# Operands of a one-column threshold and of one normalisation moved from SBUF to PSUM on VectorE

## The chip, the cores and the metric

The kernel runs on one core of a Trainium2 chip. The metric is the device time of one execution in microseconds (us), lower is better.

## What is computed

The reference is one block of a transformer with modulation, on x of 8 x 1024 x 512 in fp32. Cut to what matters here:

```
mod = silu(c) @ wmod                       # six rows of 512 for each batch: sa, ca, ga, sb, cb, gb
h = layernorm(x) * (1 + ca) + sa
x = x + ga * attention(h)                  # 3 iterations, output only nonzero in a few rows (below)
h = layernorm(x) * (1 + cb) + sb
x = x + gb * (quantise(h) @ quantise(w).T + bias)

# attention, after each iteration it
diff = mean(abs(iter_out - prev))
attn_out = where(done, attn_out, iter_out)
done = done | (diff < thr + fac * diff) & (it > 0)
```

The reference slices the first 16 positions of each batch before it iterates, so attention works on 8 x 16 = 128 rows. All other rows get only a constant row from it.

## The kernel before

The work is in two strands that share the engines.

**The main strand.** The 8192 rows are cut into 64 tiles of 128 rows, in 16 groups of four (`TILES = 4`). ScalarE normalises (`normalise`, line 474) and sums; GpSimd multiplies and adds the modulation in half groups of 128 x 1024 (`times_c`, line 379; `plus_sb`, line 390) and takes the quantised values back from the grid (`from_grid`, line 366); VectorE finds the block maxima (1215) and puts values on the grid (1234). For each tile TensorE turns the values (`transposes`, line 724), ScalarE takes the high part of them (`high_part`, line 454), VectorE the low part (`low_part`, line 1196), and TensorE multiplies in 12 matmuls (`product`, line 746). VectorE multiplies the result by the gate (`times_gate`, line 1255) and adds it to x (`add_tile`, line 1261), and ScalarE then presets the freed PSUM bank with the bias (`preset`, line 463).

**The head.** The 128 attention rows are worked on in small steps between the tiles. Each engine has one loop, `for q in range(LAST)`, with q from 0 to 63, and calls `head_work(q)` in it. The passes of the attention are `attend(i, o)`: pass i (0 to 2), step o, with q = 9 + 15 i + o. After them comes the head's own second half, at q = `AFTER` + n with `AFTER` = 51.

**Order.** Every engine's order is written out by hand and engines wait for each other by semaphores. VectorE carries out its instructions in order: in each q it does `times_gate(q - 1)`, `low_part(q + 1)`, `add_tile(q - 1)`, the group's grid work, and last `head_work(q)`. So what `head_work(q)` takes delays the three tile steps of q + 1. TensorE's `transposes(n)` waits for `low_part(n - 2)`, in the loop of q = n - 2. `link` marks an instruction whose end VectorE waits for before the next.

**The places that the change touches.**

- *The threshold*, step o = 14 of pass 1, q = 38, lines 1129 to 1137. TensorE has summed the differences into column 0 of `bb` (PSUM bank 7). Four instructions on one column make `dn[:, 2]` (the mean difference), `dn[:, 3]` (the bound), `dn[:, 6]` (1 if the difference is under the bound) and `dn[:, 7]` (one less that). `dn` is in SBUF. The two flags are read in pass 2, o = 12 (lines 1121 and 1123). TensorE waits for `dn_step` in pass 2, o = 0, before it overwrites `bb`.
- *The head's second normalisation*, q = 55 and 56, lines 1173 to 1180. `xs` (SBUF, 128 x 512) holds the head's x, `bb` the projected attention, `msp` (SBUF) the modulation rows, `mv` mean and variance, `hs` (SBUF) the result, which `quantise` takes at q = 57. `xs` is read again by GpSimd at the end (line 431).
- `own` is PSUM bank 5, which holds VectorE's small scratch values.

Of the kernel before, what the change touches and what calls it, by code (L numbers as in the profile page):

```python
# [9 lines left out]
ALU = mybir.AluOpType  # L10
# [3 lines left out]
B, T, D = 8, 1024, 512  # L14
HEADS, HD, E, ITERS = 16, 32, 16, 3
# [22 lines left out]
def build(nc, x, xh, WqT, WkT, WvT, WoT, bo, lna, BDs, rows, columns, masks, w, bias, cT, wmod, ident, out):  # L38
# [4 lines left out]
    with ExitStack() as ctx:  # L43
# [94 lines left out]
        s64 = own[:, 0:64].rearrange("p (h n) -> p h n", h=2)  # L138
        inv = own[:, 64:128].rearrange("p (h n) -> p h n", h=2)
        rsp, lmax, ksum, qrs = own[:, 128:128 + TILES], own[:, 144:160], own[:, 160:176], own[:, 176:192]  # L140

        def by_column(a):
            return a.rearrange("p (n b) -> p n b", b=B)
# [493 lines left out]
        def _(pe):  # L637
# [147 lines left out]
            def attend(i, o):  # L785
                if o == 0:
                    pe.wait_ge(q_ready, i + 1)
                    pe.wait_ge(kT_ready, i + 1)
                    M(ba, BD[:, 0, :], qT, start=True, stop=True).then_inc(qc_mm, 1)
                    if i == 0:  # L790
                        pe.wait_ge(cleared, 4)
                        pe.wait_ge(bd_done, 8)
                        pe.wait_ge(lrow_done, 5)
                    if i == 2:
                        pe.wait_ge(dn_step, 1)
                    project(bb, kT, 2, 1, kc_mm)
                elif o == 1:
                    pe.wait_ge(qc_cp, 2 * i + 2)
                    for c in range(NC):
                        m = M(ba[:, 4 * c:4 * c + 4], sq[:, 0, c * P:(c + 1) * P], col[:, GM:GM + 4],  # L800
                              start=True, stop=True)
                    m.then_inc(vq_mm, 1)
                elif o == 4:
                    pe.wait_ge(kn_done, i + 1)
                    turn(bb, kn, knT_mm)
                    pe.wait_ge(vT_ready, i + 1)
                    project(ba, vT, 3, 2, vn_mm)
                elif o == 6:
                    pe.wait_ge(knT_cp, i + 1)
                    pe.wait_ge(vn_cp, i + 1)  # L810
                    M(ba, mkr[:, 0:P], mkr[:, P:P + D], start=True, stop=False, skip_group_check=True)
                    logits(i, 0)
                    if i < ITERS - 1:
                        M(bb, BD[:, 1, :], kT, start=True, stop=True).then_inc(kv_mm, 1)
                    logits(i, 1)
                elif o == 7:
                    logits(i, 3)
                elif o == 8 and i < ITERS - 1:
                    pe.wait_ge(kT_ready, i + 2)
                    M(bb, BD[:, 3, :], vT, start=True, stop=True).then_inc(kv_mm, 1)  # L820
                elif o == 11:
                    pe.wait_ge(eT_done, i + 1)
                    if i < ITERS - 1:
                        pe.wait_ge(vT_ready, i + 2)
                    for h in range(HEADS):
                        for j in range(4):
                            r = slice(32 * j, 32 * j + 32)
                            m = M(bb[r, 32 * h:32 * h + 32], eT[r, h % 4, h // 4, :], vn[r, 32 * h:32 * h + 32],  # L828
                                  start=True, stop=True)
                    m.then_inc(pv_mm, 1)  # L830
                elif o == 13 and i < ITERS - 1:
                    pe.wait_ge(ai_done, i + 1)
                    turn(ba, cur[i], aiT_mm)
                    if i == 1:
                        pe.wait_ge(dsum_done, 1)
                        M(bb[:, 0:1], ones[:], dn[:, 0:1], start=True, stop=True).then_inc(dsum_mm, 1)
# [81 lines left out]
        def _(dve):  # L918
# [5 lines left out]
            def link(ins):  # L924
                ins.then_inc(dve_step, 1)
                chain[0] += 1
                dve.wait_ge(dve_step, chain[0])
# [134 lines left out]
            def moments(src, n):  # L1062
                link(W_.bn_stats(bn[:], src))
                link(W_.bn_aggr(mv[:], bn[:]))
                TS(st[:, 0, n:n + 1], mv[:, 1:2], EPS, None, ALU.add).then_inc(var_done, 1)
# [6 lines left out]
            def attend(i, o):  # L1072
# [14 lines left out]
                elif o == 8:  # L1087
                    dve.wait_ge(lg_mm, 4 * i + 4)
                    TT(lg, ba.rearrange("p (q c t) -> p q c t", q=4, c=NC),
                       st[:, 4, 0:16].rearrange("p (c q) -> p q c", q=4).unsqueeze(3).to_broadcast([P, 4, NC, 32]),  # L1090
                       ALU.mult).then_inc(lg_step, 1)
                    flat = lg.rearrange("p q c t -> p (q c) t")
                    dve.wait_ge(lg_step, 2 * i + 1)
                    RED(lmax, flat, AX, ALU.max).then_inc(lg_step, 1)
                    dve.wait_ge(lg_step, 2 * i + 2)
                    TT(flat, flat, wide16(lmax), ALU.subtract).then_inc(sub_done, 1)
                elif o == 10:
                    dve.wait_ge(ex_done, i + 1)
                    W_.transpose(eT.rearrange("p q c t -> p (q c t)"),
                                 ex.rearrange("p q c t -> p (q c t)")).then_inc(eT_done, 1)  # L1100
                    RED(st[:, 6, 0:16], ex.rearrange("p q c t -> p (q c) t"), AX, ALU.add).then_inc(e_step, 1)
                    dve.wait_ge(e_step, 2 * i + 1)
                    REC(st[:, 7, 0:16], st[:, 6, 0:16]).then_inc(e_step, 1)
                elif o == 12:
                    dve.wait_ge(e_step, 2 * i + 2)
                    dve.wait_ge(pv_mm, i + 1)
                    held = bb.rearrange("p (c q d) -> p c q d", c=NC, q=4)
                    scale = st[:, 7, 0:16].rearrange("p (q c) -> p c q", q=4).unsqueeze(3).to_broadcast([P, NC, 4, HD])
                    if i == 1:

                        TT(held, held, scale, ALU.mult).then_inc(diff_done, 1)
                        dve.wait_ge(diff_done, 1)
                        W_.tensor_copy(cur[1], bb).then_inc(ai_done, 1)
                        TT(diff, bb, cur[0], ALU.subtract).then_inc(diff_done, 1)
                        dve.wait_ge(diff_done, 2)
                        RED(dn[:, 0:1], diff, AX, ALU.add, apply_absolute_value=True).then_inc(dsum_done, 1)
                    else:
                        TT(cur[i].rearrange("p (c q d) -> p c q d", c=NC, q=4), held, scale, ALU.mult).then_inc(ai_done, 1)
                        dve.wait_ge(ai_done, i + 1)
                    if i == 2:  # L1120
                        TS(bb, cur[1], dn[:, 6:7], None, ALU.mult).then_inc(keep_done, 1)
                        dve.wait_ge(keep_done, 1)
                        STT(att[:], cur[2], dn[:, 7:8], bb, ALU.mult, ALU.add).then_inc(att_done, 1)
                elif o == 14 and i < ITERS - 1:
                    dve.wait_ge(aiT_mm, i + 1)
                    TT(qT, chunked(ba), qT, ALU.add).then_inc(q_ready, 1)
                    if i == 1:
                        dve.wait_ge(dsum_mm, 1)
                        TS(dn[:, 2:3], bb[:, 0:1], 1.0 / (B * HEADS * T * HD), None, ALU.mult).then_inc(dn_step, 1)
                        dve.wait_ge(dn_step, 1)  # L1130
                        TS(dn[:, 3:4], dn[:, 2:3], col[:, FAC:FAC + 1], col[:, THR:THR + 1],
                           ALU.mult, ALU.add).then_inc(dn_step, 1)
                        dve.wait_ge(dn_step, 2)
                        TT(dn[:, 6:7], dn[:, 2:3], dn[:, 3:4], ALU.is_lt).then_inc(dn_step, 1)  # L1134
                        dve.wait_ge(dn_step, 3)
                        TS(dn[:, 7:8], dn[:, 6:7], -1.0, 1.0, ALU.mult, ALU.add).then_inc(dn_step, 1)
                        dve.wait_ge(dn_step, 4)

            def head_work(q):
                i, o = pass_of(q)  # L1140
# [29 lines left out]
                elif q == AFTER + 4:  # L1170
                    dve.wait_ge(head_mm, PROJECTED)
                    dve.wait_ge(msp2_in, 16 * B)
                    link(TT(bb, bb, msp[:, GA - 1, :], ALU.mult))
                    link(TT(xs[:], xs[:], bb, ALU.add))
                    moments(xs[:], 2)
                elif q == AFTER + 5:
                    dve.wait_ge(std_done, 3)
                    link(REC(st[:, 3, 2:3], st[:, 1, 2:3]))
                    link(STT(bb, xs[:], mv[:, 0:1], msp[:, C - 1, :], ALU.subtract, ALU.mult))  # L1179
                    link(STT(hs[:], bb, st[:, 3, 2:3], msp[:, SB - 1, :], ALU.mult, ALU.add))  # L1180
                elif q == AFTER + 6:
                    quantise(hs[:].unsqueeze(1), Qh[:].unsqueeze(1), NB).then_inc(sxd_done, 1)
# [200 lines left out]
```

## Time and profile before

| | us |
|---|---|
| median of 3 runs | 339.31 |
| lowest and highest | 336.63 and 339.8 |
| the profiled execution | 338.35 |
| its span, first to last instruction | 336.3 |
| busy in it: TensorE (matmul) | 304.5 (91%) |
| VectorE | 290.4 (86%) |
| ScalarE | 239.9 (71%) |
| GpSimd | 227.5 (68%) |
| mean granted TensorE clock | 0.974 of full |

The engines are named PE (TensorE, with PEld for its weight loads), DVE (VectorE), ACT (ScalarE), POOL (GpSimd). A timeline row gives start, duration, engine, line of the kernel, operation and operands as output<-inputs, and in brackets how long the engine had been idle before and what ended that. Times are us from the start of the span. Tile names are the program's: all PSUM banks are `ps`, and `early` holds qT.

### The profile page before, as it was taken

What the parts mean: (1) busy time and instruction counts of PE and PEld (TensorE: products, weight loads), DVE (VectorE), ACT (ScalarE), POOL (GpSimd) and SP (SyncE); (2) the same over time, 40 slices, a digit from 0 to 9 for tenths busy, and PEclk for the clock granted to TensorE, in tenths of its full rate; (3) what the DMA queues carried; (4) which work ended last, traced back from release to release, by engine and by line L of the source; (5) the groups of instructions that cost most, each with busy time, mean ns of one, the idle gap of its engine ahead of it and who ended that gap; (6) DMA issues with size and microseconds to landing.
All of it is one profiled execution on the core that took longest, in us unless ns stands there. A gap on an engine that the chain in (4) does not pass through costs nothing. (4 is left out here: it accounts for less than half of the span.)

```text
span 336.3 us, 6060 instructions
## 1 busy us (share of the span) xinstructions
PE 304.5 (91%) x2159; PEld 227.8 (68%) x2159; DVE 290.4 (86%) x512; ACT 239.9 (71%) x536; POOL 227.5 (68%) x122
## 2 busy tenths in 40 slices
PE   7879999785899989998999999996999998998993
PEld 5213547565798777786888678874787785776782
DVE  4678759979999799799989979999798899989753
ACT  3278845698679979799998989976799875322410
POOL 1449393599748886969999996977878967722100
PEclk9999998979699999999999999999799999999999
DMA  6999699999979839996899699964773693303133
GB/s 185 394 406 399 231 150 239 355 307 346 225 174 241 154 134 225 276 212 232 136 236 271 221 229 247 248 175 79 228 117 127 185 146 142 127 0 125 49 140 94
DMA packets 23971, 69.00 MB, mean 205 GB/s; under 512 B 2387, under 2 KB 2516, under 8 KB 19974
## 3 DMA queue, kind: packets, MB, share of 16 engines
q1 hardware_dynamic: 16304, 53.83, 48.0%
q0 software_dynamic: 7392, 14.68, 26.0%
q8 instruction: 17, 0.28, 0.3%
q10 hardware_dynamic: 246, 0.12, 0.2%
q14 instruction: 12, 0.10, 0.1%
HBM read 51.48 MB, written 17.14 MB: 204 GB/s over the span
## 5 line engine op out<-in xcount | busy, mean ns | idle before, releaser
L746 PE MATMUL ps<-WH,XH 128*128 128x512 f32 x256 | 108.8, 427 | 1.1 <-issue 0.9
L746 PE MATMUL ps<-WL,XH 128*128 128x512 f32 x256 | 103.3, 405 | 0.0
L379 POOL TENSOR_TENSOR U<-U,c_bc 128x1024 f32<-128x1024 f32 x31 | 74.6, 2408 | 39.0 <-ACT U L474 38.4
L390 POOL TENSOR_TENSOR U<-U,sb_bc 128x1024 f32<-128x1024 f32 x31 | 74.4, 2399 | 2.5
L746 PE MATMUL ps<-WH,XL 128*128 128x512 f32 x256 | 69.7, 394 | 0.2 <-DVE XL L1196 0.2
L463 ACT COPY ps<-bias_bc 128x512 f32<-128x512 f32 x61 | 36.0, 590 | 38.9 <-DVE X L1261 38.9
L1255 DVE TENSOR_TENSOR ps<-ps,gb_bc 128x512 f32<-128x512 f32 x64 | 44.3, 692 | 15.7 <-PE ps L746 15.6
L746 PEld LDWEIGHTS ps<-WH,XH 128*128 128x128 f32 x256 | 50.0, 195 | 11.0 <-ACT XH L454 2.0
L746 PEld LDWEIGHTS ps<-WL,XH 128*128 128x128 f32 x256 | 50.2, 196 | 10.2 <-issue 1.1
L746 PEld LDWEIGHTS ps<-WH,XL 128*128 128x128 f32 x256 | 48.9, 191 | 11.8 <-DVE XL L1196 0.7
L454 ACT ACTIVATE XH<-ps 128x512 fp32r<-128x512 f32 x64 | 37.5, 587 | 22.8 <-PE ps L724 22.7
L724 PE MATMUL ps<-idf,DD 128*128 128x128 f32 x256 | 40.1, 281 | 13.5 <-DVE DD L1243 6.9
L366 POOL TENSOR_TENSOR DD<-Q,s 128x1024 f32<-128x1024 fp8e4 x24 | 46.1, 1919 | 9.1 <-DVE Q L1234 9.1
L1196 DVE TENSOR_TENSOR XL<-ps,XH 128x512 fp32r<-128x512 f32 x64 | 43.6, 682 | 8.5 <-ACT XH L454 8.4
L474 ACT ACTIVATE U<-X,nmr,rstd 128x512 f32<-128x512 f32 x64 | 48.3, 808 | 3.0 <-DVE nmr L1208 2.6
L724 PEld LDWEIGHTS ps<-idf,DD 128*128 128x128 f32 x256 | 30.7, 144 | 22.9 <-issue 9.6
L498 ACT ACTIVATE unused<-X,negm 128x512 bf16<-128x512 f32 x64 | 45.6, 714 | 0.5
L1261 DVE TENSOR_TENSOR X<-ps,X 128x512 f32<-128x512 f32 x64 | 43.6, 681 | 0.1
L1234 DVE TENSOR_TENSOR Q<-U,ps 128x1024 fp8e4<-128x1024 f32 x32 | 38.9, 1216 | 1.7 <-issue 0.4
L487 ACT ACTIVATE unused<-X 128x512 bf16<-128x512 f32 x64 | 39.5, 621 | 0.9 <-POOL X L343 0.9
L1215 DVE TENSOR_REDUCE amax<-U 128x32 f32<-128x1024 f32 x32 | 38.8, 1211 | 0.0
L356 POOL DMA_DIRECT2D X<-mod_scratch x14 | 18.1, 1293 | 11.5 <-DMA X<-in_x 6.5
(212 smaller groups left out, 351.1 us busy)
## 6 DMA issues: line engine op xcount, KB each, us to landing
X<-in_x SPq DMA_DIRECT2D x16, 1024.0 KB, 8.6
out<-X SPq DMA_DIRECT2D x15, 1024.0 KB, 4.7
X<-mod_scratch POOLq DMA_DIRECT2D x14, 1024.0 KB, 10.9
X<-in_wmod SPq DMA_DIRECT2D x2, 1024.0 KB, 12.3
sb_bc<-mod_scratch SPq DMA_DIRECT2D x7, 256.0 KB, 8.0
c_bc<-mod_scratch SPq DMA_DIRECT2D x7, 256.0 KB, 6.6
gb_bc<-mod_scratch SPq DMA_DIRECT2D x7, 256.0 KB, 8.2
msp<-mod_scratch SPq DMA_DIRECT2D x8, 160.0 KB, 9.8
```

Source lines behind the costliest of these rows:

```text
L366: nc.gpsimd.tensor_tensor(blocks(DD[:, g % 2, HALF * h:HALF * (h + 1), :]), blocks(Q8[:, h]), s32[:, g % 2, h, :].unsqueeze(2).to_broadcas ...
L379: nc.gpsimd.tensor_tensor(a, a, spread(c_bc[:, b % 2, :]), ALU.mult).then_inc(u_done, 2 if g == 0 else 1)
L390: nc.gpsimd.tensor_tensor(a, a, spread(sb_bc[:, b % 2, :]), ALU.add).then_inc(h_done, 2 if g == 0 else 1)
L474: A.activation(U[:, g % 2, j, :], X1[:, g % XSLOTS, j, :], ACT.Identity, bias=nmr[:, g % 2, j:j + 1], scale=rstd[:, g % 2, j:j + 1]).then_ ...
L487: A.activation(unused[:, j % 2, :], X1[:, g % XSLOTS, j, :], ACT.Identity, accum_out=total[:, j:j + 1]).then_inc(sum_done, 1)
L498: A.activation(unused[:, j % 2, :], X1[:, g % XSLOTS, j, :], ACT.Square, bias=negm[:, g % 2, j:j + 1], accum_out=ss[:, j:j + 1]).then_inc( ...
L724: m = TR(ps[:, XT_BANK + n % 2, c * P:(c + 1) * P], DD[:, g % 2, j, c * P:(c + 1) * P], idf[:])
L746: return M(bank, a[:, k * P:(k + 1) * P], w[:, k, :], start=False, stop=last, skip_group_check=n >= 3)
L1196: TT(XL[:, n % 2, :], ps[:, XT_BANK + n % 2, :], XH[:, n % 3, :].bitcast(F32), ALU.subtract).then_inc(xl_done, 1)
L1234: TT(blocks(Q8[:, h]), blocks(U[:, g % 2, HALF * h:HALF * (h + 1), :]), wide(inv[:, h, :]), ALU.mult, saturate=False).then_inc(q_done, 1)
L1255: TT(bank, bank, gb_bc[:, b % 2, :], ALU.mult).then_inc(scaled, 1)
L1261: TT(a, ps[:, Y_BANKS[n % 3], :], a, ALU.add).then_inc(o_done, 1)
```

## The change

Three columns of `own` get the names `change`, `bound` and `closer`. The threshold's difference is written twice, to `dn[:, 2]` and to `change`; the bound is computed from `change` into PSUM; the comparison has the bound as its tensor and `dn[:, 2]` as a per-partition scalar; its result goes to PSUM and a copy of it to `dn[:, 6]`. `dn_step` counts two more, and TensorE waits for 2 in place of 1. In the second normalisation the sum x + attention is written to `bb` in place of `xs`, its moments are taken from `bb`, a copy brings it to `xs`, and the first scalar_tensor_tensor reads `bb` in place of `xs`.

```diff
+        change, bound, closer = own[:, 400:401], own[:, 401:402], own[:, 402:403]
...
                     if i == 2:
-                        pe.wait_ge(dn_step, 1)
+                        pe.wait_ge(dn_step, 2)
                     project(bb, kT, 2, 1, kc_mm)
...
                         TS(dn[:, 2:3], bb[:, 0:1], 1.0 / (B * HEADS * T * HD), None, ALU.mult).then_inc(dn_step, 1)
-                        dve.wait_ge(dn_step, 1)
-                        TS(dn[:, 3:4], dn[:, 2:3], col[:, FAC:FAC + 1], col[:, THR:THR + 1],
-                           ALU.mult, ALU.add).then_inc(dn_step, 1)
+                        TS(change, bb[:, 0:1], 1.0 / (B * HEADS * T * HD), None, ALU.mult).then_inc(dn_step, 1)
                         dve.wait_ge(dn_step, 2)
-                        TT(dn[:, 6:7], dn[:, 2:3], dn[:, 3:4], ALU.is_lt).then_inc(dn_step, 1)
+                        TS(bound, change, col[:, FAC:FAC + 1], col[:, THR:THR + 1], ALU.mult, ALU.add).then_inc(dn_step, 1)
                         dve.wait_ge(dn_step, 3)
-                        TS(dn[:, 7:8], dn[:, 6:7], -1.0, 1.0, ALU.mult, ALU.add).then_inc(dn_step, 1)
+                        TS(closer, bound, dn[:, 2:3], None, ALU.is_gt).then_inc(dn_step, 1)
                         dve.wait_ge(dn_step, 4)
+                        W_.tensor_copy(dn[:, 6:7], closer).then_inc(dn_step, 1)
+                        TS(dn[:, 7:8], closer, -1.0, 1.0, ALU.mult, ALU.add).then_inc(dn_step, 1)
+                        dve.wait_ge(dn_step, 6)
...
                     link(TT(bb, bb, msp[:, GA - 1, :], ALU.mult))
-                    link(TT(xs[:], xs[:], bb, ALU.add))
-                    moments(xs[:], 2)
+
+                    link(TT(bb, bb, xs[:], ALU.add))
+                    moments(bb, 2)
                 elif q == AFTER + 5:
                     dve.wait_ge(std_done, 3)
                     link(REC(st[:, 3, 2:3], st[:, 1, 2:3]))
-                    link(STT(bb, xs[:], mv[:, 0:1], msp[:, C - 1, :], ALU.subtract, ALU.mult))
+                    link(W_.tensor_copy(xs[:], bb))
+                    link(STT(bb, bb, mv[:, 0:1], msp[:, C - 1, :], ALU.subtract, ALU.mult))
```

## Rows read from the trace of the kernel before

**Rows 1.** The page: granted clock in 40 slices, and the chain's shares by engine.

```profile
PEclk9999998979699999999999999999799999999999
PE 22%; DVE 9%; issue 3%; ACT 2%; DVEq 0%
```

**Rows 2.** The timeline around the threshold, 225 to 242 us.

```profile
225.82 0.15 DVE L1129 TENSOR_SCALAR dn<-ps 128x1 f32<-128x1 f32 x1
...
226.00 0.28 DVE L1131 TENSOR_SCALAR dn<-dn,col 128x1 f32<-128x1 f32 x1
226.06 2.37 POOL L379 TENSOR_TENSOR U<-U,c_bc 128x1024 f32<-128x1024 f32 x1 [2.15 <-ACT U L474]
226.31 2.13 DVE L1134 TENSOR_TENSOR dn<-dn 128x1 f32<-128x1 f32 x1
...
228.57 2.36 POOL L390 TENSOR_TENSOR U<-U,sb_bc 128x1024 f32<-128x1024 f32 x1
228.67 0.70 DVE L1255 TENSOR_TENSOR ps<-ps,gb_bc 128x512 f32<-128x512 f32 x1
...
230.01 0.66 PE L724 MATMUL ps<-idf,DD 128*128 128x128 f32 x4 [1.03 <-DVE XL L1196]
...
230.59 0.59 ACT L463 COPY ps<-bias_bc 128x512 f32<-128x512 f32 x1 [2.98 <-DVE X L1261]
...
235.97 1.18 PE L800 MATMUL ps<-col,sq 128*128 128x4 f32 x8 [2.56 <-ACT sq L508]
...
241.93 0.70 DVE L1255 TENSOR_TENSOR ps<-ps,gb_bc 128x512 f32<-128x512 f32 x1 [2.40 <-PE ps L746]
```

**Rows 3.** Stretches: length, then busy us (instructions) of PE, PEld, DVE, ACT, POOL, then granted clock, DMA share and GB/s.

```profile
118.00:122.00 4.00, 3.15 (x16) 2.69 (x17) 3.86 (x8) 3.14 (x9) 4.00 (x2) 1.00 0.48 190
...
237.00:240.00 3.00, 3.00 (x10) 2.55 (x11) 2.49 (x5) 2.97 (x8) 3.00 (x2) 0.50 0.85 236
```

**Rows 4.** The chain that ended last in order of time, 237 to 245 us.

```profile
237.15 0.95 PE ps L724 x4
238.10 3.79 PE ps L746 x12
241.89 0.44 PE ps L724 x4
242.33 2.77 PE ps L746 x12
```

**Rows 5.** The timeline around the second normalisation, 303 to 309 us.

```profile
303.47 2.50 DVE L1179 SCALAR_TENSOR_TENSOR ps<-xs,mv,msp 128x512 f32<-128x512 f32 x1
303.50 1.91 POOL L366 TENSOR_TENSOR DD<-Q,s 128x1024 f32<-128x1024 fp8e4 x1 [4.09 <-DVE Q L1234]
...
306.01 0.75 DVE L1180 SCALAR_TENSOR_TENSOR hs<-ps,st,msp 128x512 f32<-128x512 f32 x1
306.79 0.70 DVE L1255 TENSOR_TENSOR ps<-ps,gb_bc 128x512 f32<-128x512 f32 x1
...
308.14 0.66 PE L724 MATMUL ps<-idf,DD 128*128 128x128 f32 x4 [1.43 <-DVE XL L1196]
```

**Rows 6.** The timeline: VectorE instructions with a PSUM operand while GpSimd works.

```profile
119.76 2.42 POOL L390 TENSOR_TENSOR U<-U,sb_bc 128x1024 f32<-128x1024 f32 x1
...
120.84 0.23 DVE L1085 TENSOR_SCALAR st<-ps,tsc 128x16 f32<-128x16 f32 x1
...
216.59 1.91 POOL L366 TENSOR_TENSOR DD<-Q,s 128x1024 f32<-128x1024 fp8e4 x1
...
217.10 0.69 DVE L1113 COPY odd<-ps 128x512 f32<-128x512 f32 x1
```

**Rows 7.** TensorE's timeline: an earlier idle time of the engine.

```profile
118.85 0.66 PE L724 MATMUL ps<-idf,DD 128*128 128x128 f32 x4 [1.70 <-DVE XL L1196]
```

**Rows 8.** VectorE's groups by shape: busy us and mean ns after the bar.

```profile
L1063 DVE BATCH_NORM_STATS2 bn<-xs 128x6 f32<-128x512 f32 x2 | 1.4, 691 | 0.0
L1063 DVE BATCH_NORM_STATS2 bn<-ps 128x6 f32<-128x512 f32 x1 | 0.7, 699 | 0.0
```

## The prediction, made before the changed kernel ran

> **What bounds the kernel now.** I read the page first, then the chain of waits in order of time, then the timeline around the two places that the diff touches. TensorE is the engine that the kernel waits for: it has the largest share of the chain that ended last [rows 1], and where it stands still the time is lost for good, because one product follows the other up to the end of the span. So for each edit the question is whether TensorE stands still because of it. It does at both places.
>
> At the threshold a comparison of a single column takes 2.13 us, from 226.31 to 228.44. GpSimd's instruction began at 226.06 and took 2.37, so it ended at 228.43 [rows 2]. One column is no work (its neighbours take 0.15 and 0.28), so the comparison waited for GpSimd to finish. It is the only one of the four that reads two tensors from SBUF. Behind it on VectorE stand the gate product, the low part and the add of the next tile. TensorE stands still for 1.03 us until that low part is there, ScalarE for 2.98 until the add is, and as ScalarE is then late with the square that pass 2 needs, TensorE stands still again, for 2.56 until 235.97 [rows 2]. Then TensorE's clock falls to its lower level (0.50 granted, 1.2 GHz) between 237 and 240 [rows 3], and four transposes take 0.95 and a product's 12 matmuls 3.79 us, where those that follow take 0.44 and 2.77 [rows 4].
>
> At the second normalisation the scalar_tensor_tensor of two SBUF tensors takes 2.50 us; its twin with one PSUM tensor takes 0.75. GpSimd worked from 303.50 to 305.41. The low part behind it is late, and TensorE stands still for 1.43 [rows 5].
>
> **The change part by part: the threshold.** From the start of the first instruction to that of the next gate product it took 228.67 - 225.82 = 2.85 us [rows 2]. Afterwards there are six instructions.
> - The two that write the difference (`dn[:, 2]` and `change`) have no wait between them: 0.09 for the first and 0.18 for the second. The 0.18 is the distance from the first to the second start now, 226.00 - 225.82; the 0.09 is my estimate for one that is not waited for, half of that (bounds 0 and 0.18).
> - `bound`, with two per-partition scalars from SBUF, 0.31, the distance 226.31 - 226.00 [rows 2].
> - `closer`, with one per-partition scalar from SBUF and its tensor in PSUM: 0.23 plus 0.04 until the next start = 0.27. The nearest row is such an instruction on 16 columns, which took 0.23 while GpSimd was in the middle of an instruction (119.76 to 122.18) [rows 6]. So this form did not wait.
> - The copy to `dn[:, 6]`, 0.09, and the last, 0.19 (228.67 less the end of the comparison, 228.44, less 0.04 for the start).
>
> The sum is 0.09 + 0.18 + 0.31 + 0.27 + 0.09 + 0.19 = 1.13, so VectorE is free 2.85 - 1.13 = 1.72 earlier. Bounds: with each unwaited one at 0.18 it is 1.54; with them at nothing, 1.90.
>
> What does that give TensorE? The first idle time of 1.03 goes, as 1.72 is more. The other arrives through ScalarE: it waited 2.98 for the add and had nothing else to do, then worked without a break until the square, so all of this comes 1.72 earlier, and the matmuls at 235.97 start at 234.25. TensorE, which had won 1.03 before, now waits 2.56 - (1.72 - 1.03) = 1.87. The win at this point is 1.72. VectorE is no bound afterwards: at 241.93 it waits 2.40 for TensorE [rows 2].
>
> TensorE's wait for `dn_step` 2 in place of 1 costs nothing: TensorE has the rest of a product and the query projection ahead of this wait. If that cover were gone it would cost the 0.09 to 0.18 of the second write.
>
> **The clock.** It fell after an idle time of 2.56 and eight matmuls of 4 columns. With 1.87 in its place the nearest row is the idle time of 1.70 before 118.85 [rows 7], in a stretch whose clock stayed at 1.00 [rows 3], and there is the 1.43 before 308.14, where the page's slices show no fall either [rows 1, 5]. 1.87 is much nearer to 1.70 than to 2.56, so I take it that the clock stays up. What comes back is (0.95 - 0.44) + (3.79 - 2.77) = 1.53 us [rows 4]; bounds 0 (it falls all the same) and 1.53. It reaches the end, since the chain in these rows is TensorE's alone.
>
> **The second normalisation.** From 303.47 to the next gate product at 306.79 it took 3.32 [rows 5]. Afterwards: the copy of 128 x 512 from PSUM, 0.69 by its like, which did not wait though GpSimd was working from 216.59 to 218.50 [rows 6], plus 0.04 = 0.73; the first scalar_tensor_tensor, now with one SBUF tensor, 0.78 as its twin (306.79 - 306.01); and the twin itself, 0.78. The sum is 2.29 and the win 1.03. TensorE's idle time of 1.43 shrinks to 0.40, so all 1.03 arrives. Writing the sum to `bb` in place of `xs` at q = 55 costs nothing: it is one instruction with one PSUM and one SBUF tensor as before, and the moments cost 699 in place of 691 ns [rows 8]. The added copy is the price here; without it the win would be 1.76, of which TensorE could take 1.43.
>
> A rule of the Trainium skill speaks against the change: the page "VectorE: DVE Perf Modes", section "The TRN2 errata — SBUF-src ops pay a fixed extra latency per instruction", has 120 cycles fixed for a VectorE instruction from PSUM and 58 from SBUF, at 0.96 GHz. By it, as an estimate, the five instructions that change their source would each cost 0.065 us more, 0.32 in all. The rows show 8 ns for the moments from the one and the other [rows 8], so here the measurement decides.
>
> **The sum.** 1.72 + 1.53 + 1.03 = 4.28 us off the profiled execution's 338.35 (span 336.3 and 2.05 around it) gives 334.1. The median of the runs shown is 339.31, that is 0.96 above the profiled one, and with that the forecast is 335.0.
>
> **The rivals.**
> - *The clock falls all the same.* Both stalls go, but after the idle time of 1.87 and the eight matmuls the clock falls as it does now, or the runs' median did not have the loss to begin with (they differ by 3.2 us, and the fall may be part of that). For it: the idle time shrinks but does not go. Against it: 1.70 left the clock up [rows 3, 7]. The win is 2.75: 336.6.
> - *The win at the threshold doesn't arrive.* Something else is ready only later: GpSimd's next multiply waits for ScalarE and would come 1.72 earlier as well, but GpSimd's instruction before it lasts until 230.93 [rows 2]; a group's work that began late there would make the tiles of a later group late. Against it: TensorE and not GpSimd ended the waits between 237 and 245 [rows 4]. Then only 1.03 is left: 338.3.
> - *The other side: instructions with one tensor in SBUF wait as well.* Then at the threshold one of the small ones waits until 228.43 as now, and the next waits through GpSimd's following instruction, 228.57 to 230.93 [rows 2]: the gate product starts at about 231.1, 2.4 later. At the normalisation the copy takes the 2.50 and both others follow at 0.78 each, so 0.8 later than now. Together 3.2 slower: 342.5. It decides from the first instruction that waits; with no second wait it would be about even. Against it are both pairs of [rows 6]. The change then would not do what its wording says.
>
> **How the numbers follow.** Forecast 0.50, the clock falls all the same 0.33, the threshold's win doesn't arrive 0.13, the waits stay 0.04. The predicted time is the first case's, 335.0. By itself it spans 333.0 to 336.2: the unwaited instructions give 0.2 either way, and the median of a few runs whose times lie 3.2 apart moves by more than a microsecond. The range that leaves out no more than 2 in 10 reaches over the second and third case, 333.0 to 338.4. A change of 1% (3.4 us) is about what a measurement of this kernel can tell from none. Faster by over 1% is under 335.9: most of the first case (0.40) and a part of the second (0.09), 0.49. Slower by over 1% is the last case, 0.04. Within 1% is what remains, 0.47.
>
> **What the changed profile would show.** The comparison (`ps<-ps,dn`) at about 0.2 us with GpSimd in the middle of its multiply; no idle time of TensorE before the transposes that stood at 230.01; an idle time near 1.9 before the matmuls of line 800 in pass 2, and a granted clock of 1.00 behind it; products of 2.8 us there. Further on a copy of 0.69, two scalar_tensor_tensors of 0.75, and TensorE's idle time at 0.4 in place of 1.43. I would be wrong if one of the new instructions took 2 us, if TensorE's idle time moved to another place between 240 and 300, or if the granted clock still fell after pass 2 began.

## The result, and the profile after

| | before | changed |
|---|---|---|
| median, 20 executions each | 338.79 | 335.43 |
| lowest and highest | 336.63 and 339.83 | 332.6 and 339.02 |
| the profiled execution, its span | 338.35, 336.3 | 333.93, 331.9 |

The ratio of changed to before is 0.9896 (95% interval 0.9872 to 0.9921): 1% faster, 3.4 us between the medians. The ratio leaves out the changed kernel's three slowest executions (338.49 to 339.02) as slow ones; with them the means of the twenty are 338.5 and 335.6, 2.9 us apart. The profiled executions lie 4.4 us apart, and the changed kernel's times spread over 6.4 us where those of before spread over 3.2. TensorE's clock has a part in both facts, and the experiments below are mostly about it.

The timeline of the changed kernel at the threshold answers to [rows 2]:

```profile
225.77 0.15 DVE L1130 TENSOR_SCALAR dn<-ps 128x1 f32<-128x1 f32 x1
225.84 0.16 DVE L1131 TENSOR_SCALAR ps<-ps 128x1 f32<-128x1 f32 x1
...
226.02 2.38 POOL L380 TENSOR_TENSOR U<-U,c_bc 128x1024 f32<-128x1024 f32 x1 [2.18 <-ACT U L475]
226.03 0.28 DVE L1133 TENSOR_SCALAR ps<-ps,col 128x1 f32<-128x1 f32 x1
...
226.35 0.23 DVE L1135 TENSOR_SCALAR ps<-ps,dn 128x1 f32<-128x1 f32 x1
226.61 0.16 DVE L1137 COPY dn<-ps 128x1 f32<-128x1 f32 x1
226.69 0.15 DVE L1138 TENSOR_SCALAR dn<-ps 128x1 f32<-128x1 f32 x1
...
226.87 0.70 DVE L1259 TENSOR_TENSOR ps<-ps,gb_bc 128x512 f32<-128x512 f32 x1
...
227.87 1.05 PE L772 MATMUL ps<-BD,early 128*128 128x128 f32 x8
...
228.76 0.60 PE L725 MATMUL ps<-idf,DD 128*128 128x128 f32 x4
228.79 0.59 ACT L464 COPY ps<-bias_bc 128x512 f32<-128x512 f32 x1 [1.22 <-DVE X L1265]
...
234.17 1.05 PE L801 MATMUL ps<-col,sq 128*128 128x4 f32 x8 [2.06 <-ACT sq L509]
...
238.50 0.70 DVE L1259 TENSOR_TENSOR ps<-ps,gb_bc 128x512 f32<-128x512 f32 x1 [0.78 <-PE ps L747]
```

GpSimd works from 226.02 to 228.40, and all of the threshold's instructions but the first two start within that. The comparison (L1135) takes 0.23 us where it took 2.13. The way to the next gate product is 226.87 - 225.77 = 1.10 us where it was 2.85. TensorE has no idle time before the transposes at 228.76. Before line 801 it still stands idle, for 2.06 us.

The timeline at the second normalisation answers to [rows 5]:

```profile
300.01 0.69 DVE L1182 COPY xs<-ps 128x512 f32<-128x512 f32 x1
300.04 1.91 POOL L367 TENSOR_TENSOR DD<-Q,s 128x1024 f32<-128x1024 fp8e4 x1 [4.11 <-DVE Q L1238]
...
300.73 0.76 DVE L1183 SCALAR_TENSOR_TENSOR ps<-ps,mv,msp 128x512 f32<-128x512 f32 x1
...
301.53 0.75 DVE L1184 SCALAR_TENSOR_TENSOR hs<-ps,st,msp 128x512 f32<-128x512 f32 x1
...
302.31 0.70 DVE L1259 TENSOR_TENSOR ps<-ps,gb_bc 128x512 f32<-128x512 f32 x1
...
303.66 0.66 PE L725 MATMUL ps<-idf,DD 128*128 128x128 f32 x4 [0.41 <-DVE XL L1200]
```

The copy and the first scalar_tensor_tensor run in 0.69 and 0.76 us under GpSimd's instruction. It takes 2.30 from the copy to the next gate product where it took 3.32, and TensorE's idle time is 0.41 where it was 1.43.

### The profile page after: what moved, and what is told of

The parts are those of the page before. It is cut to its first block and busy times, and to the rows that moved or that the text cites. A ratio compares the mean times of both kernels' runs of the same rounds, so it can differ in the third digit from the quotient of the medians.

```text
span 331.9 us, 6063 instructions
## 1 busy us (share of the span) xinstructions
PE 302.6 (91%) x2159; PEld 226.5 (68%) x2159; DVE 287.5 (87%) x515; ACT 239.7 (72%) x536; POOL 227.4 (69%) x122
```

## The clock after pass 2 begins

The stretch from 230 to 246 us in this execution (columns as in [rows 3]) has no fall of TensorE's granted clock:

```profile
230.00:246.00 16.00, 13.94 (x77) 11.54 (x76) 14.93 (x30) 14.56 (x35) 13.85 (x8) 1.00 0.76 174
```

Three more executions of the changed kernel and one of before were profiled:

> The changed kernel itself, one look. In the profile shown, at 333.9, the granted clock stayed at 1.00 around 237 us. My theory (the same idle time of about 2 us is followed by a fall in some executions): an execution of 333 to 334 shows no fall there, one of 336 or more shows the clock at 0.50 for 3.4 or 6.9 us near 234 to 242. Rival (the slower executions differ elsewhere): an execution of 336 or more without a fall there.

> As the look before it, another execution: no fall and 333 to 334, or a fall near 234 to 242 us and 336 or more. The instructions of VectorE at the threshold and the normalisation take the same in both.

> As the two looks before it, a third execution: no fall and 333 to 334, or a fall near 234 to 242 us and 336 or more.

> The kernel before, one more look. My theory (after the longer idle time of 2.56 us the clock falls in nearly every execution, so that its times spread little): a fall to 0.50 near 237 us for 3.4 us or longer, at 337.5 to 340. Rival: no fall, and a time of 337 or less.

The changed kernel's three have two fences each here: from the timeline, TensorE's matmuls of line 801, and the stretch from 230 to 246 us. First execution:

```profile
236.36 1.05 PE L801 MATMUL ps<-col,sq 128*128 128x4 f32 x8 [2.05 <-ACT sq L509]
```

```profile
230.00:246.00 16.00, 13.95 (x78) 11.61 (x77) 14.90 (x30) 14.24 (x34) 13.82 (x8) 1.00 0.74 174
```

second execution:

```profile
233.80 1.68 PE L801 MATMUL ps<-col,sq 128*128 128x4 f32 x8 [2.06 <-ACT sq L509]
```

```profile
230.00:246.00 16.00, 13.94 (x58) 11.40 (x57) 11.90 (x24) 12.20 (x30) 10.73 (x7) 0.79 0.79 175
```

third execution:

```profile
233.28 1.05 PE L801 MATMUL ps<-col,sq 128*128 128x4 f32 x8 [2.10 <-ACT sq L509]
```

```profile
230.00:246.00 16.00, 13.90 (x67) 11.25 (x66) 13.41 (x28) 13.05 (x32) 12.22 (x8) 0.89 0.80 176
```

The idle time is the same 2.05 to 2.10 us in all four, and the granted clock afterwards is not. A mean of 0.89 over 16 us is about 3.4 us at the lower level (0.50, 1.2 GHz), 0.79 about 6.8 us: these are the lengths that stretches of 0.5 us give. What a fall costs can be read without the noise of what came earlier: from the start of line 801 (line 800 in the kernel before) to the end of the span.

| kernel | idle before line 801 | clock 230 to 246 | span - start of 801 |
|---|---|---|---|
| changed, shown | 2.06 | 1.00 | 331.9 - 234.17 = 97.7 |
| changed, 1st again | 2.05 | 1.00 | 334.1 - 236.36 = 97.7 |
| changed, 3rd again | 2.10 | 0.89 | 332.6 - 233.28 = 99.3 |
| changed, 2nd again | 2.06 | 0.79 | 334.7 - 233.80 = 100.9 |
| before, shown | 2.56 | 0.89 | 336.3 - 235.97 = 100.3 |
| before, again | 2.54 | 0.89 | 336.5 - 236.09 = 100.4 |

So no fall is 97.7, the shorter fall costs 1.6 and the longer one 3.2. The kernel before pays 1.0 more in these rows for its normalisation; without that it is at 99.3, the value with the shorter fall. What I expected of the single executions held for the second (336.82, with a fall) and for the one of before. It did not for the first, which took 335.96 without a fall here, and not for the third, which took 334.51 with one: it had reached line 801 0.9 us earlier than the execution shown.

So the spread has a second source, ahead of both places that the change touches:

| changed kernel | first gate product starts | 37th of the 64 starts | line 801 starts |
|---|---|---|---|
| shown | 52.23 | 218.99 | 234.17 |
| 1st again | 54.36 | 221.18 | 236.36 |
| 2nd again | 50.96 | 218.61 | 233.80 |
| 3rd again | 52.48 | 218.09 | 233.28 |

Ahead of the threshold (at 225.77 in the execution shown) the four lie 3.1 us apart already, nearly as far as the longer fall costs. The granted clock also falls two to four times before 93 us in every execution, at places that differ; the first again has one from about 27.5 to 31.5 us that the execution shown does not have, and is 2.13 us late at its first gate product. That this fall made it late is not shown.

## The experiments

**Each part alone.** The changed kernel with the normalisation of before:

```diff
-                    link(TT(bb, bb, xs[:], ALU.add))
-                    moments(bb, 2)
+                    link(TT(xs[:], xs[:], bb, ALU.add))
+                    moments(xs[:], 2)
...
-                    link(W_.tensor_copy(xs[:], bb))
-                    link(STT(bb, bb, mv[:, 0:1], msp[:, C - 1, :], ALU.subtract, ALU.mult))
+                    link(STT(bb, xs[:], mv[:, 0:1], msp[:, C - 1, :], ALU.subtract, ALU.mult))
```

> The threshold as changed, the normalisation as before. My theory (both stalls came from VectorE waiting for GpSimd's running instruction; TensorE's clock stays up once the first stall is gone): about 1.8 us from the shorter threshold plus 1.5 us where the granted clock no longer falls near 237 us, so 3.3 us below before; the comparison takes about 0.2 us, the scalar_tensor_tensor at the normalisation still about 2.5 us and TensorE's idle time behind it 1.4 us. Rival (the clock has no part in the gain, it falls or not by chance): about 1.8 us below before. Rival (the threshold's gain is given back): no more than 0.5 us below.

Measured: median 335.58 (333.92 to 340.2) against 338.71 of before, ratio 0.9921 (0.9885 to 0.9958), a win of 2.7 us with the interval from 1.4 to 3.9, which holds both my 3.3 and the first rival's 1.8. The spread of over 6 us is there with this part alone. The profiled execution took 338.75, and the clock fell in it although the first idle time was gone:

```profile
234.78 1.87 PE L801 MATMUL ps<-col,sq 128*128 128x4 f32 x8 [2.10 <-ACT sq L509]
```

```profile
230.00:246.00 16.00, 13.90 (x58) 11.43 (x57) 11.87 (x24) 12.26 (x28) 11.19 (x6) 0.79 0.77 175
```

Its rest of span is 336.7 - 234.78 = 101.9: 97.7, 3.2 for the longer fall, 1.0 for the normalisation, whose instruction took 2.50 as before. The theory that the clock stays up once the first idle time is gone falls with this run.

The kernel before with only the normalisation changed (the same lines the other way round):

> The normalisation as changed, the threshold as before. My theory: about 1.0 us below before, the comparison still 2.1 us, TensorE's two idle times of about 1.0 and 2.5 us behind it unchanged and the granted clock at 0.5 between 237 and 240 us. Rival (the whole gain hangs on the clock or on chance): no difference.

Measured: median 337.6 (335.64 to 339.07), ratio 0.9954 (0.9932 to 0.9977), a win of 1.6 us, interval 0.8 to 2.3. Idle times of 1.08 and 2.56, a mean clock of 0.89 from 230 to 246, and 336.5 - 237.19 = 99.3 of span behind line 800, 1.0 less than before. The 1.0 holds, and the spread stayed at 3.4 us.

**The delay without the wait.** The changed kernel with nine short instructions in PSUM behind the threshold:

```diff
                         dve.wait_ge(dn_step, 6)
+                        for n in range(9):
+                            link(TS(own[:, 403 + n:404 + n], change, 1.0, None, ALU.mult))
```

> The changed kernel with nine more one-column instructions behind the threshold, each from PSUM to PSUM and waited for, about 0.19 us each, 1.7 us in all. They can't wait for GpSimd. My theory (what costs is that VectorE's tile steps come late, whatever made them late): TensorE's idle time of about 1.0 before the next transposes and of about 2.5 before line 801 come back, with them the fall of the granted clock near 237 us; 3.3 us slower than the changed kernel. Rival (the clock has no part in it): 1.8 us slower. Rival (the wait for GpSimd costs in another way, by slowing GpSimd too): under 1 us slower.

Measured: median 337.78 (335.93 to 339.61), ratio to before 0.9973 (0.9948 to 0.9997), 2.4 us slower than the changed kernel. This is between my 3.3 and the rival's 1.8 and does not decide between them. The better comparison is the kernel before with the changed normalisation, which has about the same delay by way of the comparison: it took 337.6, and this one 337.78. Both idle times came back, and the spread shrank to 3.7:

```profile
228.88 0.66 PE L725 MATMUL ps<-idf,DD 128*128 128x128 f32 x4 [1.13 <-DVE XL L1202]
...
234.83 1.87 PE L801 MATMUL ps<-col,sq 128*128 128x4 f32 x8 [2.54 <-ACT sq L509]
```

```profile
230.00:246.00 16.00, 13.46 (x56) 11.07 (x56) 11.93 (x24) 12.31 (x29) 9.65 (x5) 0.79 0.69 159
```

So what costs is that VectorE's tile steps are late. That they had been made late by GpSimd plays no further part that these times show. The clock's fall is the longer one here, 3.2 in place of the 1.6 of before, after the same idle time: its length does not follow from the idle time alone.

**The wait itself.** The kernel before with the comparison issued twice:

```diff
+                        link(TT(dn[:, 5:6], dn[:, 2:3], dn[:, 3:4], ALU.is_lt))
                         TT(dn[:, 6:7], dn[:, 2:3], dn[:, 3:4], ALU.is_lt).then_inc(dn_step, 1)
```

> The kernel before with the one-column comparison of two SBUF tensors issued twice, each waited for. My theory (such an instruction waits until GpSimd's running instruction ends, however small it is, and if another one starts in front of it, it waits through that as well): the first takes about 2.1 us as before; the second starts just after GpSimd's instruction has ended, so it either runs in the gap in front of the next one (about 0.16 us) or waits through all of that, 2.4 us. In the second case VectorE is 2.4 us later and the kernel some 2.4 us slower, 341; in the first 0.2 us. Rival (the 2.1 us belong to the form of the instruction): both take 2.1 us and end at a time that has nothing to do with GpSimd's.

```profile
228.37 2.13 DVE L1134 TENSOR_TENSOR dn<-dn 128x1 f32<-128x1 f32 x1
230.54 0.16 DVE L1135 TENSOR_TENSOR dn<-dn 128x1 f32<-128x1 f32 x1
...
228.12 2.36 POOL L379 TENSOR_TENSOR U<-U,c_bc 128x1024 f32<-128x1024 f32 x1 [2.07 <-ACT U L474]
230.63 2.36 POOL L390 TENSOR_TENSOR U<-U,sb_bc 128x1024 f32<-128x1024 f32 x1
```

The same instruction takes 2.13 and 0.16. The first ends at 230.50, GpSimd's at 230.48; the second starts in the gap of 0.15 before GpSimd's next one and does not wait. The form by itself costs nothing, waiting for the other engine's running instruction does. The time is that of before within the interval (ratio 1.0013, 0.9988 to 1.0037), as the case of the gap foretold.

**A cheaper form of the same idea.** Only the bound goes to PSUM, and the copy to `xs` is made at q = 60, when VectorE waits for TensorE anyway; TensorE and GpSimd wait for it:

```diff
-                        TS(dn[:, 3:4], dn[:, 2:3], col[:, FAC:FAC + 1], col[:, THR:THR + 1],
+                        TS(own[:, 400:401], dn[:, 2:3], col[:, FAC:FAC + 1], col[:, THR:THR + 1],
...
-                        TT(dn[:, 6:7], dn[:, 2:3], dn[:, 3:4], ALU.is_lt).then_inc(dn_step, 1)
+                        TT(dn[:, 6:7], dn[:, 2:3], own[:, 400:401], ALU.is_lt).then_inc(dn_step, 1)
...
+                    link(STT(ba, bb, mv[:, 0:1], msp[:, C - 1, :], ALU.subtract, ALU.mult))
+                    link(STT(hs[:], ba, st[:, 3, 2:3], msp[:, SB - 1, :], ALU.mult, ALU.add))
...
+                elif q == AFTER + 9:
+                    W_.tensor_copy(xs[:], bb).then_inc(xs_kept, 1)
```

> A cheaper form of the same idea: at the threshold only the bound lies in PSUM, with four instructions as before and no second copy of the difference; at the normalisation the two scalar_tensor_tensors go through PSUM bank 6 and the copy of bank 7 to xs is made four tile steps later, at q = 60, when VectorE waits for TensorE. My theory: the threshold takes about 0.9 us in place of 1.1, and the low part behind the normalisation comes 0.7 us earlier, of which TensorE can take the 0.4 us that it still stands idle and up to 0.5 us at the next transposes. About 0.2 + 0.5 = 0.7 us (0.4 to 1.1) below the changed kernel. Rival (the added copy costs nothing since other work is late as well): no difference from the changed kernel.

Measured: median 334.69 (332.2 to 337.28), ratio to before 0.9864 (0.9819 to 0.991). Six executions do not separate that from the changed kernel. In the profiled one the same comparison as before, the only edit being that its bound lies in PSUM, ran under GpSimd's instruction:

```profile
225.75 2.38 POOL L380 TENSOR_TENSOR U<-U,c_bc 128x1024 f32<-128x1024 f32 x1 [2.18 <-ACT U L476]
226.01 0.15 DVE L1137 TENSOR_TENSOR dn<-dn,ps 128x1 f32<-128x1 f32 x1
```

0.15 us in place of 2.13, with one tensor in SBUF and one in PSUM: this is the most direct evidence that the two SBUF tensors were what made it wait. The threshold took 226.38 - 225.51 = 0.87. This execution had the longer fall (mean clock 0.79, with an idle time of only 1.84 before line 801's place), and a rest of 333.8 - 233.69 = 100.1, where 100.9 belongs to the changed kernel with that fall: 0.8 us, which fits the later copy. The six times spread over 5.1 us.

**The idle time taken away.** In step q = 40 ScalarE does two deviations of the main strand (1.6 us) before the head's square for which TensorE waits. They are moved behind it:

```diff
+                if q == BEGIN + 2 * PERIOD + 1:
+                    high_part(q + 2)
+                    head_work(q)
                 for g, h in halves(q, DEVIATE, 12):
                     deviations(g, h)
```

(and in the place further down both are left out for this q). On the changed kernel:

> The changed kernel, and on ScalarE in step q = 40 the high part and the head's two activations (lines 508 and 509) stand in front of the two deviations of the main strand. TensorE's idle time before line 801 in pass 2 should shrink from about 2.0 to 0.5 us; nothing on VectorE changes. My theory now (the changed kernel leaves an idle time of about 2 us after which the granted clock falls in some executions and not in others, for 3.4 or 6.9 us, and that makes its times spread from 332.6 to 339.0): the clock stays at 1.00 there, the median falls by the 1.5 us and by the part of the falls, to 332 to 333, and the runs lie within 2 us or so. Rival (the spread has nothing to do with this place): a median about 1.5 us below the changed kernel's 335.4, and the spread stays at 6 us.

```profile
232.56 1.05 PE L805 MATMUL ps<-col,sq 128*128 128x4 f32 x8 [0.41 <-ACT sq L509]
```

```profile
230.00:246.00 16.00, 15.59 (x87) 13.03 (x86) 15.70 (x30) 15.33 (x37) 14.65 (x8) 1.00 0.73 175
```

Measured: median 332.55 (331.28 to 334.45), ratio 0.9825 (0.9793 to 0.9856). The win over the changed kernel is 2.9 us (2.6 if each is taken against the runs of before beside it), of which 1.65 are the idle time (2.06 to 0.41). The rest, 0.9 to 1.2, fits falls that no longer happen, but no second execution was profiled to see that. The rest of span is 97.7, as without a fall.

> The same move of ScalarE's two activations on the kernel with the later copy. My theory: as the run before, and 0.5 to 0.7 us below it, 331.3 to 332.5, the fastest so far. Rival (the later copy won nothing): the same time as the run before.

Measured: median 332.36 (331.34 to 332.91), ratio 0.9811 (0.9787 to 0.9835), the fastest of all, with a spread of 1.6 us. Its rest is 329.4 - 232.41 = 97.0, that is 0.7 less than that of the run before it. The medians of six executions each lie only 0.2 apart and do not show this by themselves.

> The same move of ScalarE's two activations on the kernel before, with both long VectorE instructions left in. TensorE's idle time before line 800 in pass 2 should shrink from 2.56 to 0.8 us, the one of 1.0 us in front of it stays. My theory (the fall of the clock hangs on that idle time, not on the wait for GpSimd itself): the clock stays up, 1.7 us of idle time and about 1.5 us or more of slow matmuls go, the median about 335.0 to 335.5, and the comparison still takes 2.1 us. Rival (the clock falls all the same): about 337.0.

Measured: median 334.37 (332.03 to 337.52), ratio 0.9865 (0.9828 to 0.9903), 4.1 us below before. Idle times of 1.08 and 0.89, a mean clock of 1.00 from 230 to 246, and a rest of 330.1 - 231.37 = 98.7: no fall, and 1.0 for the normalisation. So the clock stays up in this execution with the comparison's wait left in. That move alone wins about as much as the change under study (the intervals overlap), and it touches neither of its two places. The six times spread over 5.5 us, though, and the profiled one is the fastest of them: it reached the 37th gate product, ahead of the threshold, 2.9 us earlier than the changed execution shown. Whether the slower five had a fall here is not known.

## Why the prediction was right, point by point

The time of 335.43 lies in the range and near the forecast of 335.0. But one of its three terms was too large, and the sum of 4.28 us fits the profiled pair (4.4) better than the medians (3.4). Part of the nearness is luck: the win was forecast 0.9 too large, and the median of before, 339.31 in three runs, came out 0.5 lower in twenty.

- *The comparison waited for GpSimd.* Right, and shown: the same instruction takes 2.13 and 0.16 us within one kernel, depending on GpSimd, and 0.15 under GpSimd's instruction once one of its two tensors lies in PSUM.
- *The threshold, 1.72 us.* It measured 2.85 - 1.10 = 1.75. `closer` took 0.23 with its next start 0.26 after its own (0.27 foretold); the two writes of the difference together 0.26 (0.27 foretold). At TensorE the win was 235.97 - 234.17 = 1.80, of which 0.05 was there before the threshold began (225.82 against 225.77).
- *The idle time before line 801.* Foretold 1.87, measured 2.06: TensorE gained more than its idle time of 1.03 at the first place and so came to the second wait earlier. The transposes now start at 228.76, 0.16 before the listed end of the matmuls ahead of them (227.87 + 1.05), and take 0.60 where they took 0.66: 0.22 that the prediction left out.
- *The second normalisation, 1.03.* Right in each duration (0.69, 0.76 and 0.75) and in the idle time of 0.41 (0.40 foretold). The part alone won 1.6, interval 0.8 to 2.3.
- *The clock, 1.53.* This is the step that was mis-sized. "1.87 is much nearer to 1.70 than to 2.56, so I take it that the clock stays up" drew a bound from one row on either side. After 1.84 to 2.10 us the clock stayed up in two of six profiled executions, fell for 3.4 us in one and for 6.8 us in three, so the prediction's own last sign of being wrong ("if the granted clock still fell after pass 2 began") came true in four of six. The 1.53 for one fall of the shorter length was right (1.6 measured), but the longer one costs 3.2, which was no bound of mine. Over the changed kernel's own four the fall costs (0 + 0 + 1.6 + 3.2) / 4 = 1.2 on average, against 1.6 in both profiled executions of before: a gain of 0.4 in place of 1.53. Over all six with the shortened idle time it costs 1.9, and as much over all five with 2.53 to 2.56 (1.6 four times, 3.2 in the delayed kernel): a gain of nothing. Then 1.80 + 1.03 and 0 to 0.4 make 2.8 to 3.2, beside the 3.4 between the medians and the 2.9 between the means. So few executions do not size this term more closely.
- *The rivals.* The one at 336.6 ("the clock falls all the same") is as much of the truth as the forecast: single executions go the one way or the other, and the median lies between. The two with the threshold's win lost and with further waits are out: 1.80 arrived, and neither the copy nor the scalar_tensor_tensor waited.
- *The rule on PSUM.* By the Trainium skill, "VectorE: DVE Perf Modes", section "The TRN2 errata — SBUF-src ops pay a fixed extra latency per instruction", a VectorE instruction from PSUM would, as an estimate, cost 0.065 us more than one from SBUF. The bound took 0.28 from SBUF before and 0.28 from PSUM after, the last instruction of the threshold 0.15 and 0.15, the moments 0.69 and 0.70: this kernel shows 0.01 at most.

## What to carry to other kernels

A VectorE instruction on one column that read two tensors from SBUF took 2.13 us here, until GpSimd's instruction of 2.37 had ended; look in the timeline for one-column operations of microseconds whose end falls on the end of one of GpSimd's, and put one operand into PSUM, without adding copies on the path. Then follow what was late behind it: here 1.65 of the 2.06 us that TensorE still stood idle came from ScalarE's order of work, and changing that order was worth about as much as the repair. When a shorter idle time brings the clock into play, take both of its outcomes into the sum with a chance each, and profile more than one execution.

## What was not expected

- An idle time of TensorE shortened from 2.56 to 2.06 us made the kernel's times less even: 6.4 us of spread in place of 3.2, and the fall of the clock behind it now lasts nothing, 3.4 or 6.8 us. With 0.41 or 0.19 left, no fall was seen in that place in the one profiled execution of each, and six times spread over 3.2 and 1.6. With 0.89 left, on the kernel before, no fall was seen either, yet six times spread over 5.5. So the fall is one source of the spread; how large a part it has is not shown.
- In the executions with the longer fall it began about as line 801 did (in the changed kernel's second again the mean clock is already 0.52 from 234 to 235 us, and line 801 starts at 233.80); in those with the shorter one it began 0.8 us or more after it. What decides between them was not tried.
- Three profiled executions (the changed kernel's second again, and each of the two parts alone) also had a fall near 153 us, where both kernels have an idle time of 1.6 us (1.57 and 1.56) and where the two executions shown had no fall. In the second again it came after the same 1.57, which is less than the 1.70 that the prediction took to be on the safe side:

```profile
151.28 0.38 PE L829 MATMUL ps<-late,sq 32*32 32x32 f32 x21 [1.57 <-issue]
...
152.00 0.68 PE L747 MATMUL ps<-WH,XH 128*128 128x512 f32 x1
152.48 0.63 PE L747 MATMUL ps<-WL,XH 128*128 128x512 f32 x1
```

  These matmuls took 0.47 and 0.39 in the kernel before, from 153.96. An idle time's length does not tell by itself whether a fall follows; what else does was not followed.
